# First attention of a four-stage kernel: its last four heads written out without successors, two batches scaled there, and the next stage's small constants loaded ahead of x

## The reference, cut to what matters

```python
# first attention: B=8, S=256, H=16 heads, context of L=1601 rows of 64
q_big = rope(einsum('bshk,hkq->bshq', layernorm(x) @ Wq.T, w_kc_q))
kv_r  = rope(ctx)
q_r, k_r = q_big @ W_qr, kv_r @ W_kr
attn  = softmax(einsum('bhsr,bhlr->bhsl', q_r, k_r))
ctx_c = einsum('bhsl,bld->bhsd', attn, kv_r)
x = x + einsum('bhsd,hkd->bshk', ctx_c, w_kc_kv).reshape(B, S, H*K) @ Wo.T
# then the first feed-forward: logits of layernorm(x), the top 64 rows of each batch, an MLP on these
```

## Time and profile before

| | us |
|---|---|
| median of 3 runs | 1654.04 (1652.48 to 1654.96) |
| the profiled execution's own time | 1646.0 |
| its span, first to last instruction | 1644.4 |
| granted TensorE clock, mean over the span | 0.981 of 2.4 GHz |
| PE busy | 1571.0 (96%) |
| DVE / ACT / POOL busy | 1299.1 / 1062.4 / 1153.5 |

### The profile page before, as it was taken

One profiled execution on the slowest core, in us unless ns is written; L12 is line 12 of the kernel. 1 busy time (PEld: TensorE's weight loads), 2 busy tenths in 40 slices (PEclk: granted clock), 3 DMA queues, 4 the chain that ended last, 5 costly groups with the idle time before them and its releaser, 6 DMA issues. The chain is left out here.

```text
span 1644.4 us, 50082 instructions
## 1 busy us (share of the span) xinstructions
PE 1571.0 (96%) x16337; PEld 1285.0 (78%) x16337; DVE 1299.1 (79%) x3062; ACT 1062.4 (65%) x2174; POOL 1153.5 (70%) x1102
## 2 busy tenths in 40 slices
PE   5879999999999999999999999999899889999998
PEld 4658888888888888888888888888787545555887
DVE  6978888888888888888888888888684668885323
ACT  5877777777777777777777777777222366664121
POOL 5439999999999999999999999999100224431321
PEclk8599999999999999999999999999999999999999
DMA  9721121121122122112112113412840011101344
GB/s 258 244 83 49 49 82 46 48 74 51 48 63 68 40 62 68 48 52 81 47 47 83 40 54 107 94 48 79 208 98 1 7 42 65 66 8 54 101 148 161
DMA packets 184952, 126.23 MB, mean 77 GB/s; under 512 B 107578, under 2 KB 172008, under 8 KB 184512
## 3 DMA queue, kind: packets, MB, share of 16 engines
q1 hardware_dynamic: 183360, 121.53, 26.8%
q0 software_dynamic: 1536, 3.99, 0.7%
HBM read 82.24 MB, written 24.48 MB: 65 GB/s over the span
## 5 line engine op out<-in xcount | busy, mean ns | idle before, releaser
L1243 POOL TENSOR_TENSOR c_rest<-c_prob 128x1024 f16<-128x1024 f32 (+1 forms) x513 | 817.2, 1609 | 44.4 <-ACT c_prob L1011 24.8
L1011 ACT ACTIVATE c_prob<-c_psS,ln,c_exp_scale 128x1024 f32<-128x1024 f32 (+1 forms) x514 | 528.3, 1040 | 163.4 <-PE c_psS L826 154.2
L1132 DVE TENSOR_REDUCE c_mxp<-c_psM 128x1 f32<-128x400 f32 (+1 forms) x1040 | 572.1, 571 | 52.6 <-PE c_psM L810 36.9
L826 PE MATMUL c_psS<-c_q,c_kk 128*128 128x256 f16 (+1 forms) x3350 | 513.1, 273 | 0.5 <-DVE c_ropeA L1091 0.4
L844 PE MATMUL c_psV<-c_vb,c_prob 128*128 128x129 f16 (+1 forms) x3328 | 420.8, 221 | 1.0 <-ACT c_acc L1077 1.0
L847 PE MATMUL c_psV<-c_vb,c_rest 128*128 128x65 f16 (+1 forms) x3328 | 394.8, 193 | 0.0
L826 PEld LDWEIGHTS c_psS<-c_q,c_kk 128*128 128x128 f16 (+1 forms) x3350 | 310.7, 99 | 62.1 <-issue 1.0
L810 PE MATMUL c_psM<-c_kkm,c_q 128*128 128x400 f16 (+1 forms) x1040 | 347.9, 335 | 3.5 <-DVE c_mxp L1132 2.9
L847 PEld LDWEIGHTS c_psV<-c_vb,c_rest 128*128 128x128 f16 (+1 forms) x3328 | 302.9, 98 | 29.5
L844 PEld LDWEIGHTS c_psV<-c_vb,c_prob 128*128 128x128 bf16 (+1 forms) x3328 | 312.6, 98 | 9.5 <-ACT c_acc L1077 1.2
L2221 ACT ACTIVATE g_prob<-g_psS,g_bias 128x128 f32<-128x128 f32 (+1 forms) x256 | 103.8, 426 | 49.8 <-DVE g_bias L2271 49.8
(11 more groups left out here) (336 smaller groups left out, 2448.7 us busy)
## 6 DMA issues: line engine op xcount, KB each, us to landing
c_w2s<-w_scr SPq DMA_DIRECT2D x67, 256.0 KB, 2.7
c_ms<-m_scr SPq DMA_DIRECT2D x67, 192.0 KB, 2.5
c_w2s<-w_scr SPq DMA_DIRECT2D x66, 128.0 KB, 2.0
acc_scr<-c_acc SPq DMA_DIRECT2D x129, 64.0 KB, 2.0
kv<-acc_scr SPq DMA_DIRECT2D x16, 512.0 KB, 6.4
m_w<-in_L_ffn_W SPq DMA_DIRECT2D x16, 352.0 KB, 3.5
c_vb<-V SPq DMA_DIRECT2D x27, 129.0 KB, 2.0
c_kk<-KK SPq DMA_DIRECT2D x27, 128.0 KB, 2.0
```

Of the source, the lines that this page charges most:

```text
L826: mm = pe.matmul(psS[g % 2][0:r, i * S:(i + 1) * S], src[:, (lo + i) * P:(lo + i) * P + r], mov[slot][:, :], start=(one == 0 and i % 2 == ...
L1011: nc.scalar.activation(prob[g][0:r, 0:w], psS[g % 2][0:r, 0:w], ACT.Exp, bias=keep["ln1024"][0:r, :], scale=exp_scale[slot][0:r, :]).then_ ...
L1132: nc.vector.tensor_reduce(mxp[:, st, c:c + 1], psM[:, st, 0:CHUNKS[c][1]], AX.X, ALU.max).then_inc(mx_done, 1)
L1243: nc.gpsimd.tensor_tensor(rest[g][0:r, 0:w], prob[g][0:r, 0:w], high[0:r, 0:w], ALU.subtract).then_inc(rest_done, 1)
```

## The change

Every engine's loop runs one round less, and the last four heads (124 to 127) stand behind it as plain code. There, work for heads 128 and 129 and for pairs 64 to 66 is left out, and so are SP's refills and the waits that belonged to them. Two further edits go with it. DVE, behind its last `join`, inverts the sums of seven batches instead of one, and scales batches 0 and 1 instead of batch 0 alone; the next stage scales from batch 2 on. And the next stage issues the five small constants ahead of x.

```diff
@@ sync engine, attention
                 four(H0 // AHEAD - 2, x=following)
-                four(H0 // AHEAD - 1, last=following)
+                if not ends:
+                    four(H0 // AHEAD - 1, last=following)
...
-            batch_steps(B - 1, 0)
-            sp.wait_ge(summed, 2 * N + 2)
-            sp.dma_start(t["acc_scr"][N], acc[1][:, :, DC:2 * DC]).then_inc(sent[1], 16)
+            batch_steps(B - 1, 0, ends=True)
+            for n in range(N - AHEAD, N + 1):
+                sp.wait_ge(summed, 2 * n + 2)
+                sp.dma_start(t["acc_scr"][n], acc[(n + 1) % 2][:, :, DC:2 * DC]).then_inc(sent[(n + 1) % 2], 16)
@@ tensor engine
-            with pe.Fori(0, N // AHEAD) as j:
+            with pe.Fori(0, N // AHEAD - 1) as j:
...
+            for u in range(AHEAD):
+                n, s1, s2 = N - AHEAD + u, (u + 1) % AHEAD, (u + 2) % AHEAD
+                scores(n, 2, u, (6, 8))
+                scores(n, 3, u)
+                values(n, 0, (0, 1))
+                if n + 2 < N:
+                    maxima(n + 2, (n + 2) // 2, 0, s2)
+                values(n, 0, (1, 2))
+                if n + 1 < N:
+                    pe.wait_ge(mcol_done, 2 * n + 4)
+                    shift(n + 1)
+                values(n, 0, (2, 4))
+                if n + 1 < N:
+                    scores(n + 1, 0, s1, (0, 4))
...
@@ scalar engine: the same for exp, shift_copy and the drain, without casts of queries
@@ vector engine
-            with dve.Fori(0, N // AHEAD) as j:
+            with dve.Fori(0, N // AHEAD - 1) as j:
...
-            dve.wait_ge(summed, 2 * H0 + 2)
-            first = keep["rec"][:, 1:H0 + 1, :]
+            for u in range(AHEAD - 1):
+                n = N - AHEAD + u
+                join(n + 1)
+                if n + 2 < N:
+                    for k in range(PASSES):
+                        if k == PASSES - 1:
+                            scale_of(n + 2, (u + 2) % AHEAD)
+                        reduce_max(n + 2, k)
+            dve.wait_ge(summed, 2 * (B - 1) * H0 + 2)
+            first = keep["rec"][:, 1:(B - 1) * H0 + 1, :]
             nc.vector.reciprocal(first, first).then_inc(inverted, 1)
             dve.wait_ge(inverted, 1)
-            dve.wait_ge(keep["in_acc"][0], 32)
-            for s in range(ST):
-                scale_heads(nc.vector, keep, 0, s)
+            for b in range(2):
+                dve.wait_ge(keep["in_acc"][b], 32)
+                for s in range(ST):
+                    scale_heads(nc.vector, keep, b, s)
@@ gpsimd
-            with pool.Fori(0, N // AHEAD) as j:
+            with pool.Fori(0, N // AHEAD - 1) as j:
...
+            for n in range(N - AHEAD, N):
+                rest_of(n, 1)
+                rest_of(n, 2)
+                rest_of(n, 3)
+                total(n, (n + 1) % 2)
+                if n + 1 < N:
+                    rest_of(n + 1, 0)
             total(N, 1)
@@ next stage, sync engine
-            sp.dma_start(x[:], t["x"].rearrange("b (s p) d -> p (b s) d", p=P)).then_inc(in_x, 16)
             sp.dma_start(br[:], t["L0_ffn_b_r"].partition_broadcast(P)).then_inc(in_c, 16)
...
             sp.dma_start(base[:], t["cap_base"]).then_inc(in_c, 16)
+            sp.dma_start(x[:], t["x"].rearrange("b (s p) d -> p (b s) d", p=P)).then_inc(in_x, 16)
@@ next stage, vector engine
-            later = keep["rec"][:, H0 + 1:B * H0 + 1, :]
+            later = keep["rec"][:, (B - 1) * H0 + 1:B * H0 + 1, :]
...
-                if b + 1 < B:
+                if 0 < b < B - 1:
                     scale_batch(dve, nc.vector, b + 1)
```

More of the change, by code:

```diff
@@ L721, in step, with batch_steps @@
                     refill_values(sp, last, 3)
-            def batch_steps(b, following):
+            def batch_steps(b, following, ends=False):
                 def four(j, last=None, x=None):
@@ L970, in _ @@
                     maxima(n + 2, p2, 7, s2)
+            for u in range(AHEAD):
[12 more added lines that the diff above has]
+                    scores(n + 1, 0, s1, (0, 4))
+                values(n, 1, (0, 2))
+                if n + 2 < N:
+                    maxima(n + 2, (n + 2) // 2, 1, s2)
+                elif n + 1 < N:
+                    pe.wait_ge(shift_done, n + 2)
+                if n + 1 < N:
+                    scores(n + 1, 0, s1, (4, 8))
+                if n + 2 < N:
+                    maxima(n + 2, (n + 2) // 2, 2, s2)
+                values(n, 1, (2, 4))
+                if n + 2 < N:
+                    maxima(n + 2, (n + 2) // 2, 3, s2)
+                if n + 1 < N:
+                    scores(n + 1, 1, s1, (0, 2))
+                values(n, 2, (0, 1))
+                if n + 2 < N:
+                    maxima(n + 2, (n + 2) // 2, 4, s2)
+                if n + 1 < N:
+                    scores(n + 1, 1, s1, (2, 6))
+                if n + 2 < N:
+                    maxima(n + 2, (n + 2) // 2, 5, s2)
+                if n + 1 < N:
+                    scores(n + 1, 1, s1, (6, 8))
+                values(n, 2, (1, 4))
+                if n + 2 < N:
+                    maxima(n + 2, (n + 2) // 2, 6, s2)
+                values(n, 3)
+                if n + 1 < N:
+                    scores(n + 1, 2, s1, (0, 6))
+                if n + 2 < N:
+                    maxima(n + 2, (n + 2) // 2, 7, s2)
         @block.scalar
@@ L1007, in exp @@
                 act.wait_ge(s_full, 4 * n + g + 1)
-                act.wait_ge(in_kk[(g + 2) % 4], 32 * ((n + (g + 2) // 4) // H0) + 32)
+                if not (isinstance(n, int) and n + (g + 2) // 4 == N):
+                    act.wait_ge(in_kk[(g + 2) % 4], 32 * ((n + (g + 2) // 4) // H0) + 32)
                 act.wait_ge(pv_done, 4 * n + g + 1)
@@ L1056, in _ @@
             q_other(1, 2)
-            with act.Fori(0, N // AHEAD) as j:
+            with act.Fori(0, N // AHEAD - 1) as j:
                 for u in range(AHEAD):
@@ L1080, in _ @@
                         rope_high(p, slice(2, 3), ropedR)
+            for u in range(AHEAD):
+                n = N - AHEAD + u
+                exp(n, 2, u)
+                if n + 1 < N and u % 2 == 0:
+                    shift_copy(n + 1, (u + 1) % AHEAD)
+                exp(n, 3, u)
+                if n + 1 < N and u % 2 == 1:
+                    shift_copy(n + 1, (u + 1) % AHEAD)
+                if n + 1 < N:
+                    exp(n + 1, 0, (u + 1) % AHEAD)
+                    exp(n + 1, 1, (u + 1) % AHEAD)
+                act.wait_ge(pv_done, 4 * n + 8)
+                act.wait_ge(sent[u % 2], 16 * (n // 2) + 16)
+                nc.scalar.activation(acc[u % 2][:].rearrange("p s w -> p (s w)"), psV[:, 0:ST * W],
+                                     ACT.Copy).then_inc(pv_drained, 1)
         @block.vector
@@ L1128, in reduce_max @@
                 dve.wait_ge(mx_full, PASSES * n + k + 1)
-                if st == 0:
+                if st == 0 and not (isinstance(n, int) and n + (c + 1) // len(CHUNKS) == N):
                     dve.wait_ge(in_kkm[(c + 1) % len(CHUNKS)],
```

14 lines of the change are left out of this document (6 added, 8 removed).

## The result

The changed kernel takes 1648.01 us, the kernel before 1652.43 on the same chip (medians of six runs each): ratio 0.9971, 95% interval 0.9961 to 0.9982, so 4.8 us faster (3.0 to 6.4), more than the 3.3 us that count here as no change. In a second comparison on another chip it was 1644.56 against 1649.86, ratio 0.9966 (0.9955 to 0.9978). The forecast was a gain of 2.8 us and 1651.2, "same" its likeliest case. The gain is 2 us larger. The time itself lies at the low end of the stated range (1647.8 to 1654.6), and part of that is chance: the forecast subtracts from 1654.04, and the six runs of before have a median of 1652.43.

What follows compares the result with a forecast made beforehand. PE sets the attention's pace, POOL close behind; DVE bounds the next stage's start. Tail 2.2, boundary 0.4, next stage 1.3, less 1.1 for the clock: 2.8 us off the median 1654.04, 1651.2; range 1647.8 to 1654.6.

Steps and rivals of the forecast that it cites:

- What bounds, and the tail: Attention's end: PE sets the pace, POOL next; heads 7.0 us apart, tail 21.75 instead of 28.1, 6.3 us gained if undisturbed.
- The scales: Attention's tail: DVE's four scales and POOL take turns, each delaying POOL 1.07 us, 4.1 in all; tail gains 2.2.
- The rival without turn-taking: Tail: DVE's scales cost POOL nothing or fall into its gaps; gain 6.9 us, 1647.1; chance 0.15.
- The boundary: Attention to next stage: DVE is done long before and SP has fewer waits; gain 0 to 0.6 us, taken 0.4.
- The next stage: Its start: x issued at 4.0 us, landing at 13.8; `project(1, 0)` at 14.3, 1.3 us earlier, less 1.1 for the clock.
- x lands early: Next stage: x lands at 12, PE idles under 2 us, the clock stays up; gain some 5.0 us, 1649.0; chance 0.17.
- The clock: PE's lower clock around the next stage's start costs between 0 and 1.4 us; taken 1.1.
- the first of the two ways that I named: Clock falls in heads 126 and 127: last matmuls cost 0.9 us more, slower first projections hide in the wait for x.
- The table load: Next stage, ACT: the table for the square root, formerly in DVE's way, is loaded while x travels.
- x late: Next stage: batch 2's heads mix with x, `project(1, 0)` starts at 19.2, 3.6 us later; 1656.4; chance 0.10.
- the pause at the loop's end: Leaving the loop costs each engine a pause, one to 2.5 us, so 1653; chance 0.08.

Runs made afterwards that it cites:

- the run with fillers behind the values: The changed kernel with 18 added matmuls of 128x512 f16, which nobody reads, on PE behind its last values; 4.3 us (2.5 to 5.9) faster than before.

## Why the forecast was wrong where it was

**What bounds, and the tail: right.** With the scales out of the way `total(127)` starts 20.83 us after `total(124)` (forecast 20.75), and the whole tail would be about 21.9 us by the estimate above (forecast 21.75): 6.2 gained instead of 6.3. Heads follow at 7.08 (forecast 7.0). No run has the written-out heads alone, so this part is read from the traces and not from a run of its own.

**The scales: the mechanism right, the sum too large.** The hold per scale is 0.98 to 1.03 (forecast 1.07). But I put all four on the path in full. The fourth fell on `total(127)`, ahead of a wait for ACT, where about 0.4 of it counts: 3.4 us instead of 4.1. So the tail gains 2.76 instead of 2.2. What I had not seen is the other side: the scales do not alternate with POOL. Two of the four fell on `rest_of(127, 3)` and `total(127)`, and not on `rest_of(127, 0)` and `(127, 1)`: the third waited 6 us, through three subtractions, and this is why the last came so late. The rival without turn-taking is out.

**The boundary: right,** 0.52 against 0.4.

**The next stage is the step that failed.** I summed 1.3 less 1.1 and got 0.2; it gave 2.2. Two terms:
- x's issue, the larger one. I took 4.0 us for the five constants, from rows where they stood behind x. Right behind x's own issue they are slow (the first took 1.13, 1.45 and 1.72 us in the traces of before, 2.24 in the run with x first). Ahead of x they take 0.34 to 0.43 each, and x left at 2.27. It took 9.7 to land, as forecast (9.8; but 9.4 and 8.3 in the other traces of before), so it was there at 11.97, not 13.8. With the clock held, `project(1, 0)` started 12.7 us after the stage's start, where I had 14.3: this term is 2.9 us instead of 1.3. This is the number of my rival "x lands early", 0.17 of the chance, with a gain of 5.0; its reason (a faster transfer) was another.
- The clock. I let it cost 0 to 1.4 and took 1.1, as a price on `project(1, 0)`. It fell in the tail, the first of the two ways that I named, with 3.65 us for `turn(0)` and 7.73 for the projections, and this took the place of the wait for x. By the run with fillers behind the values it costs 0.4. In the first trace of before the same fall had cost 1.4 on `turn(1)`, on the path. The second trace of before had it at the stage's start instead, where it hid in the wait for the scales as it nearly hides here, and `spread(0)` came 1.4 us earlier; the third had it at both places. So the 1.4 that I took over from one trace was not a property of the kernel, and a price is not the same at another place.

The table load did not move into the wait for x: it came at 1165.87, behind `columns(1, 0)`, which stands ahead of it in ACT's list. It ended at 1167.15, 0.5 us after DVE's aggregates, so 0.5 us of it still lay in DVE's way. It cost nothing, since PE came later still.

**A term that nobody could read off:** 1.24 us in the second attention, where the clock falls in before and not in the changed kernel. It came back with four of the variants (132.03 to 132.30 us in the stretch), three of them with fillers, so it does not follow from this change as such. What decides it stays open. It is nearly half of what the tail gained, and no part of the forecast's account.

**The rivals.** x late and the pause at the loop's end did not happen: the first head written out follows at 7.08. Of the two that would have been faster, x early came true in its time.

## What to carry to other kernels

Take an edit's price at the place where it will stand: an issue behind a large transfer, or a low clock ahead of a wait, cost something else in front of it. Where POOL sets the end, keep DVE's instructions with two SBUF inputs out of its way until its last one, or put them in a wait that exists; do not make them longer. Compare stretch by stretch over several traces before the total of one profile, or the clock in one stretch of it, is believed.

## What the chip showed that I had not expected

- A DVE instruction can be locked out over several POOL instructions: 7.20 us for one scale of 1.18, while POOL ran three subtractions from 1140.93 to 1146.5 without a gap. Where two subtractions followed each other as closely at 1137.86, a scale did get in between.
- The hold lasts for the whole of the other's instruction, also on a small one: copies of 0.18 us took 1.18, a `total` 1.43 or, beside a long scale, 2.50.
- x on a second queue, beside the constants, raised their 2.3 us to 7.3, and x's 9.7 to 11.3.
- The same work up to the last values kept the full clock in one trace and lost it at the same place, about 19.5 us after `total(124)`, in three. And in five versions that were 1.3 to 2.8 us ahead, a later fall of the clock lasted longer and took 1.3 back, but not in the two that were 4 us ahead.
- In the last stage a standstill of up to 7 us, with waits of 3.9 to 6.7 us marked "remote", in ten of the fifteen traces of the changed kernel and the variants and in none of the three of before.
